# First expert product from 12-bit parts in short float32, b2 on TensorE, keys by transposes: one change to a fused token, attention and expert kernel

## The chip, the cores and the metric

The kernel runs on one core of a Trainium2 chip. The metric is the device time of one execution in microseconds (us). PE is TensorE, DVE VectorE, ACT ScalarE, POOL GpSimd, SP SyncE, which here only issues transfers. The matmul clock of PE has two levels, 1.2 and 2.4 GHz.

## What is computed

Sixteen images (3 x 112 x 112) become 50 tokens each (49 patches and a class token) of width D = 192, through a patch convolution, a wavelet branch and depthwise convolutions. With 128 text tokens each sequence has T = 178 tokens. Then two residual layers follow:

```python
h = h + attn(layernorm(h))            # 12 heads of 16, own token masked, softmax
h = h + ffn(layernorm(h))
# ffn: logits = gamma * zscore_last(q @ k.T * scale); probs = softmax(logits)
x = layernorm(src + probs @ v @ Wo.T + bo) * ln1_g + ln1_b
gate = softmax(x @ Wg.T + bg)         # 4 experts
combine = gate where it is among the two largest, else 0
hid = relu(x @ W1[e] + b1[e])         # 192 -> 768, for every expert e
y = hid @ W2[e] + b2[e]               # 768 -> 192
out = layernorm(x + sum_e combine[e] * y[e]) * ln2_g + ln2_b
```

All four experts are computed for every token; combine weighs them. Everything is to hold to about float32, since the choice of the two largest gates hangs on it.

## The kernel before, in words

**Stages.** A first block (0 to 156 us) makes the image tokens of all 16 images. The second block works on eight pairs of images. A pair's 2 x 178 tokens lie in three tiles of 128 partitions, the third with the 2 x 50 image tokens; transposed they are 370 columns (XN) of two halves of 96 rows (HC).

**Rounds.** A round works on three or four pairs at once: a in the second part of attention of layer 1 (stage 0), b in the attention of the ffn (stage 1), nxt entering layer 1, and m, the pair before b, in its expert layer. Two rounds without m run first, then a loop of five (`Fori`), then two rounds written out with their own fill tables (FILL_A7, FILL_B7), and a last one that holds nothing but the expert layer of pair 7. Each engine has its own program of the same round and meets the others by semaphores. The order on PE in `pe_round` is: turn xn[1], query, key and value of stage 1, `pe_deviation`, the pass for the maxima and the exponential pass of stage 0, the pass for the maxima of stage 1, output of stage 0, exponential pass and output of stage 1, turn, query and key of nxt, what is left of the experts, the transposes of x2 (L930), value of nxt (L736), the gate (L940).

**The expert layer as fill.** An expert layer has 24 units of 128 hidden channels (UNITS, six for an expert). `MOE_STEPS` is 49: step 2u is the first product of unit u (L615: two float32 products with K = 96, W1 as weights, x2T as the moving side, into bank 4 or 5), step 2u + 1 is the second product of unit u - 1 (L627: three products of hid with w2, summed over an expert's six units in banks 6 and 7). ACT makes hid (L640, relu with b1) in between. DVE adds comb[e] times the sum into acc behind every sixth unit (`expert`, L650) and gives the banks back by y_used. The table FILL says how many steps stand at each named point of the round; the rest (`moe.rest()`) follow after the key of nxt. Steps are the same on every engine, and each engine does its own part of them in its own order.

**b2.** `MoeDve.start` (L667) sets acc to x2 plus the four rows of b2 weighted by comb, in twelve instructions, right behind xc.

**A float32 product.** In the trace each float32 matmul is two records of weight load and matmul; a transpose and a bfloat16 matmul are one.

**The round's end on DVE.** In `dve_round` stand in this order: output of stage 1 (L1260, L1263), the norm of x2 (14 small steps and the products with ln1_g and ln1_b), the norm of h1 (`dve_norm1`), the splits of q32 and k32 of nxt into three bfloat16 parts (L1107 to L1110), what is left of the experts (expert 3), value of nxt (L1117), `dve_gate` (L1269 and on: softmax and the choice of two), `finish` (L678 to L694: the last norm, into fin). The next round begins with the mean of xT[1] (L1180) and xc = xT[1] - mean (L1186), on which PE's key product of stage 1 waits.

**Deviation.** The z-score of the logits needs the sum over keys of the squared centred logit. `pe_deviation` makes the centred keys a second time with tokens on partitions (`pe_tokens`, L736, six float32 products), ACT copies them (kct, L1016 to L1018), PE forms G = K'K for each image (L855), DVE masks it by head (L1201), PE multiplies it with q (L861), DVE with q again (L1207), PE sums within heads (L867).

**Weights.** w1 and w2 (2304 KB each) are loaded by SP in the first block. POOL only copies: the image tokens of the next pair into h0 (L1347), h1 into its keeps. SP stacks the parts of q and k through DRAM (`stack`, L1380 and L1384) and the rows of maxima (L1390).

## Time and profile before

| what | us |
|---|---|
| three runs | 1362.61, 1373.47, 1376.96 |
| their median | 1373.47 |
| profiled execution, span from first to last instruction | 1371.2 |
| PE busy | 1171.5 |
| DVE busy | 698.9 |
| ACT busy | 432.5 |
| POOL busy | 52.9 |

The profiled execution is told by its span; no own time of it is printed beside that. Busy time of PE is the union of its matmul records, and the end of a record is modelled with its latency, so that from one start to the next is the better measure of what a group takes. The mean granted clock of PE over the span is 0.881 of full speed. Idle time in brackets names what ended it; "issue" is time in which the engine waited for nothing that the profile shows.

### The profile page before, as it was taken

Reading aid. Unit: us, or ns where it says so; the run is one execution under the profiler, and the core shown is the slowest. Engines: PE = TensorE matmul, PEld = TensorE weight load, DVE = VectorE, ACT = ScalarE, POOL = GpSimd, SP = SyncE. Lnnn points to the kernel's source line nnn. Section 1 sums busy time; section 2 is a strip of 40 time slices with the busy share of each in tenths; the row PEclk is TensorE's granted clock in tenths of the full one; section 3 lists DMA queues with packets and bytes.
Section 4 is the critical chain, followed back from the end, with each engine's and each line's share of the span. In section 5 each row is a group of like instructions: output and inputs, shape, how many; then the busy total and the mean of one; then the engine's idle time right before and its main releaser. Section 6 shows DMA issues by size and latency. Waiting matters only on the chain.

```text
span 1371.2 us, 19879 instructions
## 1 busy us (share of the span) xinstructions
PE 1171.5 (85%) x7172; PEld 790.7 (58%) x7172; DVE 698.9 (51%) x1981; ACT 432.5 (32%) x933; POOL 52.9 (4%) x89
## 2 busy tenths in 40 slices
PE   7798546586789998999899989998999999885996
PEld 4343324353457666757666766575667756662775
DVE  3467742544275357535743574466456652724242
ACT  1222103132324342434242425332533343241321
POOL 6101100000000000000000000000000000000000
PEclk9999656566789998999898999998999999996998
DMA  9200040232031204210421043004301520012000
GB/s 277 88 1 0 7 78 1 47 76 40 8 78 40 41 7 88 54 33 1 88 58 29 1 94 66 15 15 87 65 10 25 101 41 2 9 39 40 1 8 8
DMA packets 37991, 60.55 MB, mean 44 GB/s; under 512 B 4976, under 2 KB 30176, under 8 KB 37344
## 3 DMA queue, kind: packets, MB, share of 16 engines
q1 hardware_dynamic: 35504, 55.86, 19.4%
q10 hardware_dynamic: 2384, 3.30, 0.8%
q8 instruction: 66, 1.08, 0.4%
q14 instruction: 37, 0.30, 0.1%
HBM read 42.36 MB, written 16.34 MB: 43 GB/s over the span
## 4 chain that ended last, share of the span: by engine, by line
PE 55%; DVE 19%; issue 9%; ACT 4%; DMA 2%; SPq 1%; DVEq 0%; POOL 0%; ACTq 0%; POOLq 0%
PE PS L615 13%; PE PS L627 11%; PE PS L736 6%; PE PS L822 5%; PE PS L763 5%; PE PS L728 4%; DVE mx L1227 3%; PE PS L769 3%; PE PS L778 2%; PE PS L831 2%; ACT probs L994 1%; PE PS L837 1%; PE PS L855 1%; PE PS L867 1%; DVE rem L1108 1%
## 5 line engine op out<-in xcount | busy, mean ns | idle before, releaser
L615 PE MATMUL PS<-x2T,w 96*128 96x370 f32 x768 | 289.8, 504 | 7.2 <-issue 7.2
L627 PE MATMUL PS<-w,hid 128*128 128x192 f32 x1152 | 233.9, 342 | 7.9 <-ACT hid L640 7.6
L627 PEld LDWEIGHTS PS<-w,hid 128*128 128x128 f32 x1152 | 205.4, 201 | 47.3 <-issue 12.6
L640 ACT ACTIVATE hid<-PS,b 128x370 f32<-128x370 f32 x192 | 108.8, 568 | 383.0 <-PE PS L615 383.0
L1227 DVE TENSOR_REDUCE mx<-PS 128x2 f32<-128x356 f32 x288 | 129.8, 520 | 148.5 <-PE PS L763 105.4
L615 PEld LDWEIGHTS PS<-x2T,w 96*128 96x128 f32 x768 | 146.9, 201 | 68.5 <-issue 18.8
L994 ACT ACTIVATE probs<-PS 128x356 f32<-128x356 f32 x288 | 112.8, 485 | 29.5 <-PE PS L763 19.3
L763 PE MATMUL PS<-kst,qst 96*128 96x178 bf16 x384 | 69.5, 276 | 32.8 <-DMA kst<-scr_k 14.2
L728 PE MATMUL PS<-xT,w_at 96*96 96x370 f32 x192 | 77.1, 552 | 8.8 <-ACT q L961 5.2
L778 PE MATMUL PS<-masks,ident_bf 128*128 128x256 bf16 (+1 forms) x288 | 79.8, 278 | 0.0
L650 DVE SCALAR_TENSOR_TENSOR acc<-PS,comb,acc 128x192 f32<-128x192 f32 x96 | 34.0, 409 | 86.9 <-PE PS L627 86.9
L822 PE MATMUL PS<-probs,va 128*32 128x178 f32 x1536 | 71.4, 328 | 6.7 <-ACT probs L994 6.7
L763 PE MATMUL PS<-qst,kst 99*128 99x178 bf16 x384 | 57.4, 252 | 17.2 <-DMA qst<-mrows 13.2
L1248 DVE RECIPROCAL rs<-PS 128x36 f32<-128x36 f32 x16 | 6.1, 383 | 129.2 <-PE PS L831 129.2
L763 PEld LDWEIGHTS PS<-kst,qst 96*128 96x128 bf16 x384 | 27.5, 105 | 67.0 <-DVE mx L1227 31.1
L736 PE MATMUL PS<-w_at,oT 96*128 96x192 f32 x288 | 55.8, 347 | 4.4 <-ACT oT L1011 4.4
L728 PEld LDWEIGHTS PS<-xT,w_at 96*96 96x96 f32 x192 | 35.2, 187 | 42.0 <-issue 10.6
L822 PEld LDWEIGHTS PS<-probs,va 128*32 128x32 f32 x1536 | 46.4, 112 | 22.1 <-issue 8.3
L736 PEld LDWEIGHTS PS<-w_at,oT 96*128 96x128 f32 x288 | 50.6, 202 | 8.5 <-ACT oT L1011 8.4
L763 PEld LDWEIGHTS PS<-qst,kst 99*128 99x128 bf16 x384 | 28.7, 101 | 44.8 <-issue 30.0
L371 DVE SCALAR_TENSOR_TENSOR dwo<-pad_l,chan,dwo 96x441 f32<-96x441 f32 x48 | 38.1, 793 | 14.1 <-ACT cw L295 12.6
L736 PE MATMUL PS<-w_at,xT 96*128 96x192 f32 x192 | 40.2, 366 | 5.5 <-ACT k L976 3.5
(190 smaller groups left out, 1393.0 us busy)
## 6 DMA issues: line engine op xcount, KB each, us to landing
qst<-scr_q SPq DMA_DIRECT2D x96, 144.0 KB, 4.6
scr_q<-qs SPq DMA_DIRECT2D x16, 432.0 KB, 3.3
scr_k<-ks SPq DMA_DIRECT2D x16, 432.0 KB, 4.7
kst<-scr_k SPq DMA_DIRECT2D x16, 432.0 KB, 4.8
w<-in_w SPq DMA_DIRECT2D x2, 2304.0 KB, 36.8
kst<-scr_k SPq DMA_DIRECT2D x16, 288.0 KB, 5.8
cols<-in_x_cols SPq DMA_DIRECT2D x6, 392.0 KB, 14.2
kst<-scr_k SPq DMA_DIRECT2D x16, 144.0 KB, 6.3
```

Of the source, the lines that this page charges most:

```text
L371: ch.link(nc.vector.scalar_tensor_tensor(out=out, in0=image_rows(PAD_OF[r][:, 0, :], tap_offset(t), n), scalar=col(C_DW + 18 * r + t), in1 ...
L615: ins = nc.tensor.matmul(PS[:, 4 + u % 2, 0:XN], w1[:, k, 128 * u:128 * u + 128], x2T[:, k, 0:XN], start=(k == 0), stop=(k == 1))
L627: ins = nc.tensor.matmul(tile_psum((6, 7), i), hid[u % 2][:, 128 * i:128 * i + 128], w2[:, u, :], start=(j == 0 and i != 1), stop=(j == FT ...
L640: nc.scalar.activation(hid[u % 2][:, 0:XN], PS[:, 4 + u % 2, 0:XN], ACT.Relu, bias=b1[:, u:u + 1]).then_inc(S["h_ready"], 1)
L728: ins = nc.tensor.matmul(PS[0:HC, FRONT[s][m], 0:XN], w_at[:, w, k, HC * m:HC * m + HC], x[:, k, 0:XN], start=(k == 0), stop=(k == 1))
L736: ins = nc.tensor.matmul(tile_psum(banks, i), tile_cols(x, k, i), w_at[:, w, k, :], start=(k == 0), stop=(k == 1))
L763: ins = nc.tensor.matmul(PS[:, bank, T * b:T * b + T], still[0:rows_, h, TP * b:TP * b + NTXT], move[0:rows_, h, TP * b:TP * b + T], start ...
L769: ins = nc.tensor.matmul(PS[64 * b:64 * b + 64, 2, T * g:T * g + T], still[0:rows_, 2 * u + g, TP * b + NTXT:TP * b + TP], move[0:rows_, 2 ...
L778: ins = nc.tensor.matmul(own, ident_bf[:], m.rearrange("p (b j) -> p b j", b=2), start=False, stop=True, skip_group_check=True)
L822: ins = nc.tensor.matmul(PS[32 * q:32 * q + 32, 3, T * b:T * b + T], va[s][:, 2 * i + b, h, :], pr, start=(i == 0), stop=(i == 1), skip_gr ...
L994: nc.scalar.activation(probs[:, u % PROB_UNITS, bank, :], PS[:, bank, 0:T2], ACT.Exp)\
L1227: nc.vector.tensor_reduce(out, PS[:, g, 0:T2].rearrange("p (b j) -> p b j", b=2), AX.X, ALU.max)\
```

## The change

x2 is transposed to full 128 partitions: plane 0 has channels 0 to 127, plane 1 has channels 128 to 191 twice (x2_wide holds those 64 columns a second time). ACT copies the transposes to x2T_hi in the type float32r (short float32), DVE writes the remainder as x2T_lo. W1 is held as w1_hi and w1_lo (channels 0 to 127) and w1_rest (rows 0 to 63 the high part of channels 128 to 191, rows 64 to 127 their low part). A unit's first product is then five short products over 128 rows. POOL makes these tiles at the start of the second block from loads that it issues itself, in four chunks of 1536 columns, by way of qst[1]; SP's stacks of stage 1 and PE's expert rounds wait for them. The gate takes the same parts, four products for a tile in place of two, and DVE adds the two halves.

b2 goes to PE: comb is transposed (bank 4), copied by ACT into hid[0], and multiplied with b2 in banks 6 and 7, which DVE adds to acc after expert 3. MOE_STEPS is 50.

The centred keys with tokens on partitions come from eight transposes of k32 in place of `pe_tokens`. The weights of the value product have 17 columns in place of 32, and DVE clears bank 3 once. tok_gain, tstat, tmv, tsc, loc, kct and gsb lie in other tiles now; tok_gain is loaded by SP at the start of the second block, and DVE waits for it. FILL and its two variants are unchanged.

```diff
-        w1 = sb("w1", [HC, 2, E * FF])
+        w1_hi = sb("w1_hi", [128, E * FF], F32R)
+        w1_lo = sb("w1_lo", [128, E * FF], F32R)
+        w1_rest = sb("w1_rest", [128, E * FF], F32R)
...
-        va = [sb(f"va{s}", [128, 4, HEADS, 32]) for s in range(2)]
...
                 pe, m = self.eng, self.m
-                if odd:
+                if u == UNITS and odd:
+                    self.bias()
+                elif odd:
                     if u:
                         self.second(u - 1)
                 elif u == UNITS:
+                    pe.wait_ge(S["comb_ready"], at(m, 1, 1))
+                    for i in range(3):
+                        ins = nc.tensor.transpose(PS[0:E, 4, 128 * i:128 * i + 128], comb[:, i, :], ident[:])
+                    ins.then_inc(S["ct_psum"], 1)
                     self.second(UNITS - 1)
                 else:
                     if u >= 2:
                         pe.wait_ge(S["h_ready"], at(m, UNITS, u - 1))
-                    for k in range(2):
-                        ins = nc.tensor.matmul(PS[:, 4 + u % 2, 0:XN], w1[:, k, 128 * u:128 * u + 128],
-                                               x2T[:, k, 0:XN], start=(k == 0), stop=(k == 1))
+                    f = slice(128 * u, 128 * u + 128)
+                    for k, (w, x, plane) in enumerate(((w1_hi, x2T_hi, 0), (w1_lo, x2T_hi, 0), (w1_hi, x2T_lo, 0),
+                                                       (w1_rest, x2T_hi, 1), (w1_rest, x2T_lo, 1))):
+                        ins = nc.tensor.matmul(PS[:, 4 + u % 2, 0:XN], w[:, f], x[:, plane, 0:XN],
+                                               start=(k == 0), stop=(k == 4))
                     ins.then_inc(S["h_psum"], 1)
+
+            def bias(self):
+
+                pe, m = self.eng, self.m
+                pe.wait_ge(S["y_used"], at(m, E + 1, E))
+                pe.wait_ge(S["ct_ready"], at(m, 1, 1))
+                for i in range(3):
+                    ins = nc.tensor.matmul(tile_psum((6, 7), i), combT[:, 128 * i:128 * i + 128], b2[:],
+                                           start=(i != 1), stop=True, skip_group_check=True)
+                ins.then_inc(S["bias_psum"], 1)
...
                     nc.scalar.activation(hid[u % 2][:, 0:XN], PS[:, 4 + u % 2, 0:XN], ACT.Relu,
                                          bias=b1[:, u:u + 1]).then_inc(S["h_ready"], 1)
+                elif not odd:
+                    act.wait_ge(S["ct_psum"], at(m, 1, 1))
+                    nc.scalar.copy(combT[:, 0:XN], PS[0:E, 4, 0:XN]).then_inc(S["ct_ready"], 1)
 
         class MoeDve(Moe):
 
 
             def expert(self, e):
                 dve, m = self.eng, self.m
+                if e == 0:
+                    dve.wait_ge(S["comb_ready"], at(m, 1, 1))
                 dve.wait_ge(S["h_used"], at(m, UNITS, FT * (e + 1)))
                 for i in range(3):
                     ins = nc.vector.scalar_tensor_tensor(out=acc[:, i, :], in0=tile_psum((6, 7), i),
-                                                         scalar=comb[:, i, e:e + 1], in1=acc[:, i, :],
+                                                         scalar=comb[:, i, e:e + 1], in1=(acc if e else x2)[:, i, :],
                                                          op0=ALU.mult, op1=ALU.add)
                 ins.then_inc(S["y_used"], 1)
-                dve.wait_ge(S["y_used"], at(m, E, e + 1))
+                dve.wait_ge(S["y_used"], at(m, E + 1, e + 1))
+
+            def bias(self):
+                dve, m = self.eng, self.m
+                dve.wait_ge(S["bias_psum"], at(m, 1, 1))
+                nc.vector.tensor_tensor(acc[:, 0:2, :], PS[:, 6, 0:2 * D].rearrange("p (i d) -> p i d", i=2), acc[:, 0:2, :],
+                                        ALU.add)
+                nc.vector.tensor_tensor(acc[:, 2, :], PS[:, 7, 0:D], acc[:, 2, :], ALU.add).then_inc(S["y_used"], 1)
+                dve.wait_ge(S["y_used"], at(m, E + 1, E + 1))
 
             def step(self, u, odd):
-                if u and u % FT == 0 and (odd or u == UNITS):
+                if u == UNITS and odd:
+                    self.bias()
+                elif u and u % FT == 0 and (odd or u == UNITS):
                     self.expert(u // FT - 1)
-
-            def start(self):
-
-                dve, m = self.eng, self.m
-                ch = chain(dve, "dve_bias", m)
-                dve.wait_ge(S["comb_ready"], at(m, 1, 1))
-                for e in range(E):
-                    for i in range(3):
-                        ins = nc.vector.scalar_tensor_tensor(out=acc[:, i, :], in0=rows[:, R_B2 + e, :],
-                                                             scalar=comb[:, i, e:e + 1], in1=acc[:, i, :] if e else x2[:, i, :],
-                                                             op0=ALU.mult, op1=ALU.add)
-                    ch.link(ins)
-                ch.end()
 
             def finish(self):
...
+                        ins = nc.tensor.matmul(PS[32 * q:32 * q + VW, 3, T * b:T * b + T], va[s][:, 2 * i + b, h, :],
                                                pr, start=(i == 0), stop=(i == 1), skip_group_check=True)
             ins.then_inc(S["pv_psum", s], 1)
...
 
-            pe_tokens((0, 1), 5, xc, S["kc_psum"])
+            for h in range(2):
+                for b_ in range(2):
+                    o = D * b_ + HC * h
+                    nc.tensor.transpose(PS[:, 0, o:o + HC], k32[:, h, b_, 0:NTXT], ident[0:HC, 0:HC])
+                    ins = nc.tensor.transpose(PS[0:NB, 1, o:o + HC], k32[:, h, b_, NTXT:T], ident[0:HC, 0:HC])
+            ins.then_inc(S["kc_psum"], 1)
             moe.point("kc")
             pe.wait_ge(S["kc_ready"], at(b, 1, 1))
             pe.wait_ge(S["v_ready", 1], at(b, 1, 1))
-            for c in range(2):
-                for h in range(2):
-                    for i in range(2):
-                        x = kct[:, 2 * i + c, HC * h:HC * h + HC]
-                        o = HC * (2 * h + c)
-                        ins = nc.tensor.matmul(PS[0:HC, 2, o:o + HC], x, x, start=(i == 0), stop=(i == 1))
+            for h in range(2):
+                for i in range(2):
+                    for c in range(2):
+                        half = slice(HC * h, HC * h + HC)
+                        x = kct[0:NB, 2 + c, half] if i else kct[:, c, half]
+                        ins = nc.tensor.matmul(PS[0:HC, 2 + c, half], x, x, start=(i == 0), stop=(i == 1))
             ins.then_inc(S["g_psum"], 1)
             moe.point("g")
             pe.wait_ge(S["g_ready"], at(b, 1, 1))
             for h in range(2):
                 for c in range(2):
-                    ins = nc.tensor.matmul(PS[0:HC, h, T * c:T * c + T], gsb[:, 2 * h + c, :], q32[1][:, h, c, 0:T],
+                    ins = nc.tensor.matmul(PS[0:HC, h, T * c:T * c + T], gsb[:, 2 * c + h, :], q32[1][:, h, c, 0:T],
...
+            if m is not None:
+                pe.wait_ge(S["w_split"], 2 * WCH + 1)
             moe.point("start")
...
-                        ins = nc.tensor.transpose(PS[0:HC, (2, 3)[h], 128 * i:128 * i + 128], x2[:, i, HC * h:HC * h + HC],
-                                                  ident[:])
+                        ins = nc.tensor.transpose(PS[:, (2, 3)[h], 128 * i:128 * i + 128],
+                                                  x2_wide[:, i, 128 * h:128 * h + 128], ident[:])
                 ins.then_inc(S["x2T_psum"], 1)
             if nxt is not None:
                 pe_value(pe, 0, nxt)
             if b is not None:
 
-                pe.wait_ge(S["x2T_ready"], at(b, 1, 1))
+                pe.wait_ge(S["w_split"], 1)
+                pe.wait_ge(S["x2T_lo"], at(b, 1, 1))
                 for i in range(3):
-                    for k in range(2):
-                        ins = nc.tensor.matmul(PS[:, 2, E * i:E * i + E], tile_cols(x2T, k, i), gate_w[:, k, :],
-                                               start=(k == 0), stop=(k == 1))
+                    o = 2 * E * i
+                    for k, (x, plane) in enumerate(((x2T_hi, 0), (x2T_lo, 0), (x2T_hi, 1), (x2T_lo, 1))):
+                        w = gate_b[:] if plane else gate_a[:].rearrange("p c e -> p (c e)")
+                        ins = nc.tensor.matmul(PS[:, 2, o:o + (E if plane else 2 * E)], tile_cols(x, plane, i), w,
+                                               start=(k == 0), stop=(k == 3), skip_group_check=True)
                 ins.then_inc(S["gate_psum"], 1)
 
...
             nc.scalar.copy(kct[:, 0:2, :].rearrange("p i d -> p (i d)"), PS[:, 0, 0:2 * D])
-            nc.scalar.copy(kct[0:NB, 2, :], PS[0:NB, 1, 0:D])
-            nc.scalar.copy(kct[64:64 + NB, 3, :], PS[64:64 + NB, 1, 0:D]).then_inc(S["kc_ready"], 1)
+            nc.scalar.copy(kct[0:NB, 2:4, :].rearrange("p i d -> p (i d)"), PS[0:NB, 1, 0:2 * D]).then_inc(S["kc_ready"], 1)
...
-                nc.scalar.copy(x2T[:], PS[0:HC, 2:4, 0:XW]).then_inc(S["x2T_ready"], 1)
+                nc.scalar.copy(x2T_hi[:], PS[:, 2:4, 0:XW]).then_inc(S["x2T_ready"], 1)
                 act.wait_ge(S["gl_ready"], at(b, 1, 1))
...
-                ch.link(nc.vector.tensor_tensor(y[:], y[:], row(gain, 3), ALU.mult))
-                ins = nc.vector.tensor_tensor(y[:], y[:], row(gain + 1, 3), ALU.add)
+                ch.link(nc.vector.tensor_tensor(y, y, row(gain, 3), ALU.mult))
+                ch.link(nc.vector.tensor_tensor(x2_wide[:, :, D:D + DB], y[:, :, 128:D], row(gain + 1, 3)[:, :, 128:D],
+                                                ALU.add))
+                ins = nc.vector.tensor_tensor(y, y, row(gain + 1, 3), ALU.add)
             ins.then_inc(done, 1)
...
-            moe.start()
             moe.point("norm")
             moe.point("query")
...
-            nc.vector.tensor_tensor(gsb[:], PS[0:HC, 2, 0:4 * HC].rearrange("p (i c) -> p i c", i=4),
-                                    same_head[:].unsqueeze(1).to_broadcast([HC, 4, HC]), ALU.mult).then_inc(S["g_ready"], 1)
+            for c in range(2):
+                ins = nc.vector.tensor_tensor(gsb[:, 2 * c:2 * c + 2, :], PS[0:HC, 2 + c, 0:D].rearrange("p (h c) -> p h c", h=2),
+                                              same_head[:].unsqueeze(1).to_broadcast([HC, 2, HC]), ALU.mult)
+            ins.then_inc(S["g_ready"], 1)
             moe.point("g")
...
-            nc.vector.tensor_tensor(gl[:], PS[:, 2, 0:3 * E].rearrange("p (i e) -> p i e", e=E),
-                                    bg[:].unsqueeze(1).to_broadcast([128, 3, E]), ALU.add).then_inc(S["gate_used"], 1)
+            parts = PS[:, 2, 0:6 * E].rearrange("p (i c e) -> p i c e", c=2, e=E)
+            ch.link(nc.vector.tensor_tensor(gl[:], parts[:, :, 0], bg[:].unsqueeze(1).to_broadcast([128, 3, E]), ALU.add))
+            nc.vector.tensor_tensor(gl[:], parts[:, :, 1], gl[:], ALU.add).then_inc(S["gate_used"], 1)
             dve.wait_ge(S["gate_used"], at(b, 1, 1))
...
+            if b is not None:
+                dve.wait_ge(S["x2T_ready"], at(b, 1, 1))
+                nc.vector.tensor_tensor(x2T_lo[:], PS[:, 2:4, 0:XW], x2T_hi[:], ALU.subtract).then_inc(S["x2T_lo"], 1)
             if nxt is not None:
                 dve_value(dve, 0, nxt)
...
+        def split_weights(pool):
+
+            for g in range(2):
+                out = gate_b[:] if g else gate_a[:, 0, :]
+                nc.gpsimd.tensor_copy(out, gate_w[:, g, :]).then_inc(S["w_cast"], 1)
+                pool.wait_ge(S["w_cast"], g + 1)
+            nc.gpsimd.tensor_tensor(gate_a[:, 1, :], gate_w[:, 0, :], gate_a[:, 0, :], ALU.subtract).then_inc(S["w_cast"], 1)
+            pool.wait_ge(S["w_cast"], 3)
+            nc.gpsimd.tensor_tensor(gate_b[DB:128], gate_w[DB:128, 1, :], gate_b[DB:128], ALU.subtract).then_inc(S["w_split"], 1)
+            for n in range(2 * WCH):
+                rest, f = n // WCH, slice(WC * (n % WCH), WC * (n % WCH) + WC)
+                pool.wait_ge(S["w_split"], n + 1)
+                pool.dma_start(raw, a["w1_rest" if rest else "w1"][:, f]).then_inc(S["raw_in"], 16)
+                pool.wait_ge(S["raw_in"], 16 * n + 16)
+                hi = (w1_rest if rest else w1_hi)[:, f]
+                nc.gpsimd.tensor_copy(hi, raw).then_inc(S["w_cast"], 1)
+                pool.wait_ge(S["w_cast"], n + 4)
+                if rest:
+                    ins = nc.gpsimd.tensor_tensor(w1_rest[DB:128, f], raw[DB:128], w1_rest[DB:128, f], ALU.subtract)
+                else:
+                    ins = nc.gpsimd.tensor_tensor(w1_lo[:, f], raw, hi, ALU.subtract)
+                ins.then_inc(S["w_split"], 1)
+            pool.wait_ge(S["w_split"], 2 * WCH + 1)
...
+            if s:
+                sp.wait_ge(S["w_split"], 2 * WCH + 1)
             sp.wait_ge(S[f"{which}_split", s], at(r, 1, 1))
...
                 load_text(sp, 0)
...
+                pe.wait_ge(ld_moe, 16)
                 pe.wait_ge(casts, 1)
...
                 for x in (qs, ks):
```

Outside of the engines' programs: w1 is laid out as its first 128 rows and, as w1_rest, its last 64 rows twice; gate_w likewise; b2 is an input of its own and no longer part of rows.

## Rows read from the trace of the kernel before

**Rows 1.** The page: busy shares; the chain that ended last, by engine and line

```profile
PE 1171.5 (85%) x7172; PEld 790.7 (58%) x7172; DVE 698.9 (51%) x1981; ACT 432.5 (32%) x933; POOL 52.9 (4%) x89
...
PE 55%; DVE 19%; issue 9%; ACT 4%; DMA 2%; SPq 1%; DVEq 0%; POOL 0%; ACTq 0%; POOLq 0%
PE PS L615 13%; PE PS L627 11%; PE PS L736 6%; PE PS L822 5%; PE PS L763 5%; PE PS L728 4%; DVE mx L1227 3%; PE PS L769 3%; PE PS L778 2%; PE PS L831 2%; ACT probs L994 1%; PE PS L837 1%; PE PS L855 1%; PE PS L867 1%; DVE rem L1108 1%
```

**Rows 2.** Groups by form: line, shapes, count; busy us, mean ns; idle before

```profile
L615 PE MATMUL PS<-x2T,w 96*128 96x370 f32 x768 | 289.8, 504 | 7.2 <-issue 7.2
...
L667 DVE SCALAR_TENSOR_TENSOR acc<-rows,comb,acc 128x192 f32<-128x192 f32 x72 | 27.7, 439 | 0.9
...
L1110 DVE TENSOR_TENSOR qs<-rem,qs 96x712 bf16<-96x712 f32 x16 | 14.4, 898 | 0.6
...
L340 POOL TENSOR_TENSOR dwo<-dwo,cw 96x441 f32<-96x441 f32 x10 | 13.6, 1365 | 101.8 <-ACT cw L295 101.8
```

**Rows 3.** Timeline of PE, 630 to 702 us: start, us, instruction, records, [idle before]

```profile
649.16 1.41 PE L615 MATMUL PS<-x2T,w 96*128 96x370 f32 x4
650.41 2.12 PE L627 MATMUL PS<-w,hid 128*128 128x192 f32 x12
652.36 0.82 PE L930 MATMUL PS<-ident,x 128*96 128x128 f32 x6
653.02 2.12 PE L736 MATMUL PS<-w_at,xT 96*128 96x192 f32 x12
...
658.20 4.42 PE L615 MATMUL PS<-x2T,w 96*128 96x370 f32 x8 [1.84 <-issue]
...
676.20 5.25 PE L728 MATMUL PS<-oT,w_at 96*96 96x370 f32 x8 [3.77 <-DVE oT L1186]
```

**Rows 4.** Busy time by stretch: us, then PE, PEld, DVE, ACT, POOL; clock, DMA

```profile
636.00:676.00 40.00, 34.59 (x157) 25.37 (x155) 30.61 (x107) 11.80 (x25) 1.32 (x2) 0.96 0.36 75
676.00:768.00 92.00, 87.49 (x661) 59.80 (x662) 42.19 (x116) 35.65 (x81) 0.69 (x2) 0.91 0.17 33
```

**Rows 5.** Timeline of DVE, 630 to 702 us

```profile
654.68 1.06 DVE L650 SCALAR_TENSOR_TENSOR acc<-PS,comb,acc 128x192 f32<-128x192 f32 x3
...
656.99 0.17 DVE L1269 TENSOR_TENSOR gl<-PS,bg 128x12 f32<-128x12 f32 x1
...
673.25 0.68 DVE L1180 TENSOR_REDUCE xbar<-xT 96x4 f32<-96x512 f32 x1 [6.00 <-issue]
```

**Rows 6.** Timelines of DVE and PE, last three rounds

```profile
1073.62 0.42 DVE L1186 TENSOR_TENSOR oT<-xT,xbar 96x256 f32<-96x256 f32 x1
...
1076.30 2.65 PE L728 MATMUL PS<-oT,w_at 96*96 96x370 f32 x8
...
1250.83 0.75 PE L763 MATMUL PS<-kst,qst 96*128 96x178 bf16 x4 [12.01 <-issue]
...
1315.27 1.07 DVE L667 SCALAR_TENSOR_TENSOR acc<-rows,comb,x 128x192 f32<-128x192 f32 x3
...
1321.21 1.21 PE L627 MATMUL PS<-w,hid 128*128 128x192 f32 x6 [0.19 <-DVE acc L650]
```

**Rows 7.** Timelines of PE and of SP's queue, 555 to 610 us

```profile
575.41 0.49 PE L796 MATMUL PS<-ident,mpart 128*36 128x128 f32 x3 [0.62 <-DVE mpart L1236]
...
580.30 0.31 PE L763 MATMUL PS<-qst,kst 99*128 99x178 bf16 x2
...
601.29 2.67 PE L615 MATMUL PS<-x2T,w 96*128 96x370 f32 x4
...
576.48 2.36 SPq L1390 DMA_DIRECT2D qst<-mrows  x3
```

**Rows 8.** The chain, in order of time: the same step in the first round

```profile
215.73 2.05 DMA qst<-mrows
```

**Rows 9.** DMA issues: bytes of one, us from issue to landing

```profile
bands<-in_pg_bands SPq DMA_DIRECT2D x1, 576.0 KB, 5.3
```

**Rows 10.** Timeline of POOL

```profile
243.76 0.34 POOL L1347 COPY h<-img_tok 49x192 f32<-49x192 f32 x1 [81.95 <-DVE h L1263]
```

73 lines of the change are left out of this document (45 added, 28 removed).

## The prediction

> **What bounds the kernel now.** I read the page's busy shares first: TensorE (PE) is busy 85% of the span, VectorE (DVE) 51%, and the chain that ended last is 55% PE and 19% DVE, its largest line L615, the first expert product, 13% [rows 1]. So one could think that every microsecond taken from L615 is won. The groups price it: 192 units of four matmul records, 289.8 us in all [rows 2]. In the timeline the next matmul starts 1.25 us after such a unit (649.16 to 650.41), so a record streams for 0.31 us and a float32 product, two records, takes 0.62 [rows 3].
>
> Then I asked where the chain runs, round by round. A steady round (132 to 138 us) has two parts. In the first, 92 us, PE is busy 87.5 and sets the pace [rows 4]. In the second, 40 us, from stage 1's output projection to the centred keys of the next round, the chain is DVE's: x2's norm, h1's norm, four splits, expert 3, value, gate, the end of the previous pair's expert layer, 6 us in which it issues nothing (the loop's turn), then the mean and xc [rows 5]. PE only fills there and waits 3.77 us for xc, after which it runs at the lower clock level (1.2 GHz): eight records of 370 columns take 5.25 us, at the upper level 2.65 [rows 3, 6]. What PE saves in this part is worth nothing; what DVE's chain gets longer there, the round does too. That split decides the case.
>
> **The first product.** Two float32 products (1.25 us) become five short ones of the same 370 columns. No row shows the short type. From below, a product can't be cheaper than one pass over its columns, half a record, 0.155 us; from above, it could run like float32, 0.62. I take one pass, as bfloat16 does: two records of 178 columns last 0.31 us together, their latency included [rows 7]. Loads of float32 weights follow each other every 0.11 us in the six transposes from 652.36 to 653.02 [rows 3], so they stay hidden. Five passes are 0.78 us: 0.47 saved a unit, 0.92 at the lower clock, where a unit has 2.67 less the latency, 2.47 [rows 7].
>
> The Trainium skill (FP8 and Floating Point Precision, TensorE Precision Notes) says that true FP32 takes four passes through the array, and that "FP32 reduced precision" reads four bytes and truncates them. The trace agrees with the four, 0.62 being 4 x 0.155; no run here shows the other. By one pass of it the sum is the one below, by float32's own rate it would be the far end of rival B.
>
> Of the 24 units of a steady round nine stand in DVE's part: nothing. Of the other fifteen, three are cover that is wanted anyway: one before the split maxima (PE waits 0.62 us for mpart even now), two before the exponential pass. There SP issues the rows of maxima at 576.48, three issues in 2.36 us, the last lands some 2 us after it starts [rows 7, 8], so near 580.2, and the pass starts at 580.30. Three more gain 0.1 to 0.2 us each, because something else is late next: rem, the residual, the copy of oT. One runs at the lower clock: 0.9. Eight are won whole: 3.7. Together 5.1 a round, 25.5 for five steady rounds. The two rounds behind the loop, counted the same way, give 5.2 and 5.6: in the second PE waits 12 us for its query stack at 1250.83 whatever the units before it cost [rows 6].
>
> **Keys by transposes.** Twelve records of L736, 1.95 us (as from 653.02, less the latency), go. Eight transposes come, four at 0.11 and four of 50 columns, between 0.03 and 0.11, taken at 0.06: 0.7. Saved 1.25 a round, twice that in the slow first one: 11. ACT has two copies for three, inside the expert steps that cover them, and G's mask is 0.15 longer on DVE, also covered.
>
> **b2 on TensorE.** Twelve DVE instructions of 0.44 us go, 5 us with their gaps [rows 2]. In steady rounds they stand behind xc, beside PE's key product, and cost nothing now. In the last round they are on the chain, from 1315.27, ahead of expert 0 and of PE at 1321.21 [rows 6]. What comes stands in the bad part. PE's bias step waits for DVE's expert 3, and DVE gets to that only behind its splits, at 655.7 [rows 5], while PE is done with its second products at 652.4 [rows 3], and after the change at 650.9 (four units shorter, three small transposes more). Behind the waiting bias stand on PE the transposes of x2, the next pair's value product and the gate, which today run while DVE splits. Worked out on this round's times: expert 3 ends at 656.1, 0.35 later for the extra piece of x2's norm. Then on PE bias 1.0, transposes 0.65, value 1.95; beside them ACT's copy 0.8, DVE's two adds 0.9 and the new low part of x2, 128x768, 0.95 after the 0.90 of a 96x712 op [rows 2]; then the gate 1.35. At the upper clock the gate's first DVE op starts at 661.5 instead of 656.99, and has one op more: 4.8 late. But by then PE has stood idle for 5 us, and after 3.77 and after 1.84 us it came back at the lower level [rows 3]. If bias, transposes and value all run there, it is 8.4. I take 7.0: the clock comes back within the value product. From there DVE's chain to xc is unchanged. Four boundaries at 7.0; the next, where PE is last today (xc at 1074.0, PE at 1076.30 [rows 6]), 4.9; the one after 7.0; the first, with no expert layer in flight, 1.8: 41.7 us.
>
> **Last round.** Its gate is 1.9 us late, start() is gone, so PE's seventh second product comes 1.7 earlier than 1321.21; 17 more units save 7.9; PE waits some 0.5 us for DVE at two expert boundaries, comb's transposes take 0.5, and the bias stands bare before the final norm, 1.15 on PE and 0.95 on DVE. Net 6.0 saved.
>
> **Start.** Clearing a PSUM bank on DVE costs 0.6. The weights come in four loads of 768 KB beside the stacking transfers: between 0 and 5, taken 1. Their split runs on POOL: a load of 7 us (576 KB took 5.3), a copy and a subtraction of 1536 elements, 4.8 each at L340's 3.1 ns for an element (441 in 1.37 us): 16.6 a chunk, done near 228, ahead of POOL's image at 243.76 [rows 2, 9, 10] and of SP's second stack, later still. 17 weight columns for 32 in the value product: loads are hidden, 0 to 7 us gained, taken 0.
>
> **Sum:** -25.5 - 10.8 - 11 - 6.0 + 41.7 + 1.6 = -10 us. The page gives the profiled execution by its span alone, 1371.2; what lies around it I take as the 2.3 us to the middle of the three runs: 1371.2 - 10 + 2.3 = 1363.
>
> **Rivals.** A, the boundary is cheap: PE's clock holds through the wait (4.8, 2.7 and 4.8 instead of 7.0, 4.9 and 7.0) and the marginal units gain too. Boundaries 28.5, gains 57, start 1.6: -27, 1347; with no cost of the bias wait at all, 1.5 a boundary, 1327. For it: at 658.20, after 1.84 us, the clock was back within three units. Against: the idle is 5 us. B, a short product is two passes long, 0.31: a unit takes 1.54, 0.3 longer than now. It decides as soon as a short product costs more than 0.25. Some 123 units lie on PE's part of the chain: +37, the slow ones +2, boundaries +42, transposes -11, last round's start() -4, start +1.6: +68, 1441. For: a float32 record itself is two passes. At float32's rate it would be some 300 us. C, POOL's split is late. Beyond 16 us of room each microsecond delays the next pair's image, which is on the chain: with loads of 15 us, 16 late, 1379.
>
> The Trainium skill (SBUF — State Buffer, SBUF: two separate sides) says that a load issued by GpSimd starves while VectorE runs a two-port copy. No row of this trace shows such a load; it is what would bring C about.
>
> D, the boundary is dearer, 8.4 each, and the units in the exponential passes gain half, because ACT's exponentials come late: boundaries 50, gains 45, start 1.6: +7, 1380.
>
> **How the numbers follow.** A change of this kernel can be told from none beyond about 1%, 13.7 us. Forecast 0.40, A 0.30, B 0.07, C 0.07, D 0.16. All of A and a third of the forecast's case end below 1359.8: 0.42. All of B and two thirds of D: 0.18. The rest, 0.40, is within 1%. The range goes from between A's two values, 1335, to D's far side, 1388.
>
> **What would show it.** The first product has 960 records, 0.16 us apart. In a steady boundary PE idles 5 us before the bias, and DVE's gate starts some 8 us behind the end of expert 3, not 1.3. L667 is gone; PE is busy near 1070 us in a hardly shorter span. Wrong would be: records 0.3 us apart (B), a gap before POOL's image near 244 (C), a steady round under 130 us (A) or above 138 (D).

## The result, and the profile after

The changed kernel takes 1377.81 us (median of 20 runs), the kernel before 1371.45 beside it: ratio 1.0070, 95% interval 1.0041 to 1.0099, slower by 0.7% (by the two medians 0.5%). The forecast was 1363 us and a gain; the time came out on the other side of the kernel before. The profiled execution has a span of 1382.0 us for 1371.2. In what follows 0.001 of a ratio is 1.37 us. The ratios leave out runs more than 1.5% above the fastest of the same kernel, which matters for two kernels below: one run of six of e4, at 3394 us, and five of twelve of e13, at 1379 to 1382 us.

The page of the changed kernel:

```profile
span 1382.0 us, 20370 instructions
PE 1129.3 (82%) x7404; PEld 834.5 (60%) x7404; DVE 690.9 (50%) x1934; ACT 436.2 (32%) x933; POOL 78.9 (6%) x105
...
PE 51%; DVE 22%; issue 8%; ACT 4%; DMA 3%; SPq 1%; DVEq 0%; POOL 0%; ACTq 0%; POOLq 0%
...
L638 PE MATMUL PS<-x2T_hi,w_hi 128*128 128x370 f32 x192 | 93.4, 486 | 4.4 <-issue 4.4
...
L638 PE MATMUL PS<-x2T_hi,w_lo 128*128 128x370 f32 x192 | 67.6, 352 | 0.0
```

Against [rows 1], PE is busy 42 us less, not the 101 us that the forecast meant by 1070, and DVE 8 us less. Then the timeline of PE where products stand among second products at the upper clock (start, us, records):

```profile
1043.79 1.14 PE L660 MATMUL PS<-w,hid 128*128 128x192 f32 x6
1044.63 0.47 PE L638 MATMUL PS<-x2T_hi,w_hi 128*128 128x370 f32 x1
1044.93 0.33 PE L638 MATMUL PS<-x2T_hi,w_lo 128*128 128x370 f32 x1
1045.10 0.33 PE L638 MATMUL PS<-x2T_lo,w_hi 128*128 128x370 f32 x1
1045.27 0.33 PE L638 MATMUL PS<-x2T_hi,w_rest 128*128 128x370 f32 x1
1045.43 0.33 PE L638 MATMUL PS<-x2T_lo,w_rest 128*128 128x370 f32 x1
1045.60 1.14 PE L660 MATMUL PS<-w,hid 128*128 128x192 f32 x6
```

A short product is one pass, 0.17 us from start to start: rival B falls. But the second record comes 0.30 behind the first, since the first takes over from a float32 product (0.45 behind a projection of 96 rows, at 1053.26). A first and a second product take 1.81 us together (1043.79 to 1045.60) where [rows 3] have 2.22: 0.41 saved, not 0.47.

A steady boundary, PE first, then DVE:

```profile
664.78 2.04 PE L648 MATMUL PS<-b,hid 4*128 4x192 f32 x6 [4.79 <-DVE acc L688]
...
673.06 0.25 PE L982 MATMUL PS<-gate_b,x2T_lo 128*128 128x4 f32 x1
...
689.57 2.73 PE L760 MATMUL PS<-oT,w_at 96*96 96x370 f32 x8 [2.53 <-DVE oT L1231]
```

```profile
663.66 1.06 DVE L688 SCALAR_TENSOR_TENSOR acc<-PS,comb,acc 128x192 f32<-128x192 f32 x3
666.93 0.56 DVE L697 TENSOR_TENSOR acc<-PS,acc 128x384 f32<-128x384 f32 x1 [2.21 <-PE PS L648]
...
669.23 0.96 DVE L1383 TENSOR_TENSOR x2T_lo<-PS,x2T_hi 128x768 fp32r<-128x768 f32 x1 [1.48 <-ACT x2T_hi L1119]
...
673.35 0.17 DVE L1316 TENSOR_TENSOR gl<-PS,bg 128x12 f32<-128x12 f32 x1
...
686.16 0.68 DVE L1225 TENSOR_REDUCE xbar<-xT 96x4 f32<-96x512 f32 x1 [2.36 <-issue]
```

This is what was forecast: PE idles 4.79 us ahead of the bias product, comes back at the lower level (2.04 us for six records; the value product takes 3.99 us for the 2.12 of [rows 3]), and DVE's gate starts 8.6 us behind the end of expert 3 instead of 1.3. But DVE's idle time at the loop's turn, 6.00 us in [rows 5], is 2.36 here. Over four turns it was 24.6 us and is 9.3. And PE waits 2.53 us for xc, not 3.77, and the key product behind it runs at the upper level, 2.73 us for the 5.25 of [rows 3]. At the four boundaries of the loop this product took 4.24, 5.25, 2.73 and 5.25 us before, and takes 2.65 to 2.73 now.

By the copies of the pairs' images on POOL the kernel loses 6.2 us up to the first (249.99 for 243.76 [rows 10]), 3.7 in the round after it and 1.6 in the next; the four steady rounds gain 1.85 each (133.0 for 134.85); the first stretch behind the loop loses 6.4, the next two 4.3 and 0.4, and the last layer gains 4.5.

### The profile page after: what moved, and what is told of

It is laid out like the page before. It is cut to its first block, busy times and chain, and to the rows that moved or that the text cites. A ratio compares the mean times of both kernels' runs of the same rounds, so it can differ in the third digit from the quotient of the medians.

```text
span 1382.0 us, 20370 instructions
## 1 busy us (share of the span) xinstructions
PE 1129.3 (82%) x7404; PEld 834.5 (60%) x7404; DVE 690.9 (50%) x1934; ACT 436.2 (32%) x933; POOL 78.9 (6%) x105
## 4 chain that ended last, share of the span: by engine, by line
PE 51%; DVE 22%; issue 8%; ACT 4%; DMA 3%; SPq 1%; DVEq 0%; POOL 0%; ACTq 0%; POOLq 0%
PE PS L660 10%; PE PS L638 8%; PE PS L768 6%; PE PS L854 5%; PE PS L795 5%; DVE mx L1273 4%; PE PS L760 3%; PE PS L801 3%; PE PS L810 2%; PE PS L863 1%; PE PS L982 1%; DMA qst<-mrows 1%; PE PS L892 1%; PE PS L648 1%; SPq L1464 1%
## 5 line engine op out<-in xcount | busy, mean ns | idle before, releaser
L660 PEld LDWEIGHTS PS<-w,hid 128*128 128x128 f32 x1152 | 201.7, 199 | 16.1 <-ACT hid L673 5.3
L638 PE MATMUL PS<-x2T_hi,w_hi 128*128 128x370 f32 x192 | 93.4, 486 | 4.4 <-issue 4.4
L854 PE MATMUL PS<-probs,va 128*17 128x178 f32 x1536 | 70.5, 326 | 6.8 <-ACT probs L1036 6.8
L638 PE MATMUL PS<-x2T_hi,w_lo 128*128 128x370 f32 x192 | 67.6, 352 | 0.0
L638 PE MATMUL PS<-x2T_lo,w_rest 128*128 128x370 f32 x192 | 67.5, 351 | 0.0
L638 PE MATMUL PS<-x2T_lo,w_hi 128*128 128x370 f32 x192 | 67.2, 350 | 0.0
L638 PE MATMUL PS<-x2T_hi,w_rest 128*128 128x370 f32 x192 | 67.2, 350 | 0.0
L854 PEld LDWEIGHTS PS<-probs,va 128*17 128x17 f32 x1536 | 41.1, 99 | 24.6 <-issue 5.7
L688 DVE SCALAR_TENSOR_TENSOR acc<-PS,comb,acc 128x192 f32<-128x192 f32 x72 | 25.5, 409 | 58.1 <-PE PS L660 58.1
L768 PE MATMUL PS<-w_at,xT 96*128 96x192 f32 x192 | 49.9, 430 | 5.5 <-ACT k L1018 3.4
```

Of the source, the lines that this page charges most:

```text
L638: ins = nc.tensor.matmul(PS[:, 4 + u % 2, 0:XN], w[:, f], x[:, plane, 0:XN], start=(k == 0), stop=(k == 4))
L660: ins = nc.tensor.matmul(tile_psum((6, 7), i), hid[u % 2][:, 128 * i:128 * i + 128], w2[:, u, :], start=(j == 0 and i != 1), stop=(j == FT ...
L688: ins = nc.vector.scalar_tensor_tensor(out=acc[:, i, :], in0=tile_psum((6, 7), i), scalar=comb[:, i, e:e + 1], in1=(acc if e else x2)[:, i ...
L768: ins = nc.tensor.matmul(tile_psum(banks, i), tile_cols(x, k, i), w_at[:, w, k, :], start=(k == 0), stop=(k == 1))
L854: ins = nc.tensor.matmul(PS[32 * q:32 * q + VW, 3, T * b:T * b + T], va[s][:, 2 * i + b, h, :], pr, start=(i == 0), stop=(i == 1), skip_gr ...
```

## The experiments

Each of the ratios is against the kernel before, run on the same chip; in brackets the 95% interval. The changed kernel has 1.0070.

**The start.** On DVE and POOL, changed kernel:

```profile
169.58 3.48 POOL L1419 TENSOR_TENSOR w_lo<-qst,w_hi 128x1536 fp32r<-128x1536 f32 x1
169.63 3.45 DVE L144 TENSOR_SCALAR acc<-acc 128x7 int32<-128x7 int32 x1
...
178.25 1.91 POOL L1414 CAST w_hi<-qst 128x1536 fp32r<-128x1536 f32 x1 [4.32 <-DMA qst<-in_w]
178.87 2.70 DVE L1209 TENSOR_TENSOR img_tok<-img_tok,fin 128x1344 f32<-128x1344 f32 x1
180.24 4.70 POOL L1419 TENSOR_TENSOR w_lo<-qst,w_hi 128x1536 fp32r<-128x1536 f32 x1
181.49 3.84 DVE L1150 CAST qs<-q 96x712 bf16<-96x712 f32 x1
```

DVE's shift of seven numbers lasts as long as POOL's subtraction, and its cast of the queries 3.84 us.

```diff
 def split_weights(pool):
+    pool.wait_ge(S["k_split", 0], 1)
```

> The changed kernel, with POOL's split of the weights held back until DVE has split the first pair's keys; nothing else differs. Theory (POOL's casts and subtractions hold up DVE's own casts and scalar operations at the start): the three long DVE operations of the start (3.37, 2.70 and 3.77 us in the changed kernel) come back to 0.1, 1.6 and 0.5 us, the first max pass starts near 201 instead of 208, the next pair's image is copied near 244 to 246 instead of 249.99, and the whole is 5 to 7 us shorter than the changed kernel (1.007 of before becomes 1.002 to 1.003). Rival (the weight loads beside the stacking transfers cost it, or PE's clock): the three operations get short but the first max pass stays near 206 to 208. Rival (POOL late after all): the split, 52 us long, ends near 248 and the image copy waits for it, so nothing is won.

1373.85 us, 1.0035 [1.0006, 1.0065]. DVE's three operations in this run:

```profile
174.93 0.16 DVE L144 TENSOR_SCALAR acc<-acc 128x7 int32<-128x7 int32 x1
...
180.88 1.56 DVE L1209 TENSOR_TENSOR img_tok<-img_tok,fin 128x1344 f32<-128x1344 f32 x1
182.35 0.52 DVE L1150 CAST qs<-q 96x712 bf16<-96x712 f32 x1
```

From the first block's last addition into the image tokens to POOL's first image copy it is 89.6 us (159.07 to 248.68), in the kernel before 89.5, in the changed kernel 96.8. The weight loads now stand beside the stacking transfers and cost nothing, and the split ends at 234.6, 14 us ahead of the copy. So it is POOL's arithmetic that cost the start, 7 us in this stretch of the trace. The whole kernel's ratio falls by 5 us, which is no more than the two intervals allow by chance; the stretch and the three operations decide it. The copy's mark itself came at 248.68, later than expected, since in this execution everything ahead of POOL's split was already 5 to 6 us late.

The Trainium skill (SBUF — State Buffer, SBUF: two separate sides) calls the ports shared by VectorE and GpSimd "an exclusive lock, not a bandwidth split", held by whichever starts first. The trace agrees: POOL's subtraction starts at 169.58, DVE's operation at 169.63, and it takes 3.45 us for 0.16. The forecast had used that section only for DVE holding up POOL.

**The bias step.** Banks 4 and 5 are free once the last hidden units are read, so the product needn't wait for expert 3. DVE then reads it from there, and the next pair's first unit waits until DVE has:

```diff
-                pe.wait_ge(S["y_used"], at(m, E + 1, E))
                 pe.wait_ge(S["ct_ready"], at(m, 1, 1))
+                pe.wait_ge(S["h_ready"], at(m, UNITS, UNITS))
...
-                    ins = nc.tensor.matmul(tile_psum((6, 7), i), ...
+                    ins = nc.tensor.matmul(tile_psum((4, 5), i), ...
```

> The changed kernel, with the bias product put into PSUM banks 4 and 5 so that it doesn't wait for DVE's expert 3; the order of all instructions is kept. Theory (the wait ahead of the bias step is what makes the boundary dear): PE goes on at once, DVE's gate starts 4 to 5 us earlier behind the end of expert 3 (3.3 to 4.6 us behind it instead of 8.6). The two boundaries outside the loop gain 4 to 5 us each. In the loop DVE's gap at the turn was 6.15 us each before and 2.3 after the change: if it is tied to a fixed point of the round it grows back by up to 3.7 and a boundary gains about 1, total -13 us against the changed kernel; if the gap stays 2.3, total -28. Rival (the low part of x2 and the gate's four products are the cost, not the wait): gain under 6 us in all.

1351.67 us, 0.9888 [0.9830, 0.9945]: 25 us below the changed kernel, with some 9 us either way. Its boundary, PE and then DVE:

```profile
657.56 1.24 PE L650 MATMUL PS<-b,hid 4*128 4x192 f32 x6
...
664.34 0.24 PE L984 MATMUL PS<-gate_a,x2T_hi 128*128 128x8 f32 x1 [2.78 <-DVE x2T_lo L1385]
```

```profile
661.29 1.06 DVE L690 SCALAR_TENSOR_TENSOR acc<-PS,comb,acc 128x192 f32<-128x192 f32 x3
...
665.85 0.17 DVE L1318 TENSOR_TENSOR gl<-PS,bg 128x12 f32<-128x12 f32 x1 [0.56 <-PE PS L984]
...
679.79 0.68 DVE L1227 TENSOR_REDUCE xbar<-xT 96x4 f32<-96x512 f32 x1 [3.48 <-issue]
```

The gate starts 4.6 us after expert 3 begins, not 9.7 (663.66 to 673.35). The gap at the turn grew back, but by 1.4 us (3.69 for 2.33, mean of four turns), not 3.7: a steady round takes 129.75 us for 133.0, and the two stretches behind the loop gain 6.5 and 4.8.

Next, DVE forms the low part of x2 ahead of expert 3:

```diff
+            if b is not None:
+                ... x2T_lo <- PS - x2T_hi
             moe.rest()
-            if b is not None:
-                ... x2T_lo <- PS - x2T_hi
```

> As the run before it, and DVE forms the low part of x2 ahead of expert 3 and the bias additions, so that PE's gate runs beside these. By the theory of the wait it gains another 2 to 2.5 us at each of seven boundaries where the turn's gap doesn't give it back: 5 us (gap grows) to 15 us (gap stays) below the run before it. Rival: DVE now waits for ACT's copy of x2 ahead of expert 3, and nothing is won.

1343.69 us, 0.9837 [0.9787, 0.9886]: 7 us less, in the lower part of what was expected, and less than the two intervals together. Steady rounds gain only 0.9 (128.85).

And b2 back on DVE, the rest of the change kept:

```diff
-MOE_STEPS = 2 * UNITS + 2
+MOE_STEPS = 2 * UNITS + 1
+            moe.start()    # behind xc: twelve acc <- rows * comb + acc
```

> The changed kernel with b2 back on VectorE (twelve operations behind the centred keys, as before), all four with the first expert's b2 (the other three are left out, the time is the same); no transposes of comb, no bias product. The first product and the key transposes stay. By the forecast's sum: each steady boundary loses the wait for expert 3 (about 5 us won on the gate), the last round gets its 5 us back on the chain. With the gap at the loop's turn growing back: -4 in the loop, -9 outside, +4 in the last round, so about -9 against the changed kernel; with a constant gap -24. If b2 were a gain, it would be slower than the changed kernel by up to 5.

1346.14 us, 0.9833 [0.9775, 0.9891]. b2 on TensorE costs 0.0237, 32 us, with some 9 us either way. Both of my sizes (-9 and -24) were too small: the gap at the turns stays short (2.64 to 3.48). The profiled executions place the cost: 4.4 us in each steady round (133.0 for 128.6), and 18.8 us from the last image copy to the end.

**The three repairs together.**

> The changed kernel with the late split of the weights, the bias product in banks 4 and 5, and the low part of x2 ahead of expert 3. If the two causes are separate, the gains add: e3 stood at 0.984 of before, the late split gave 0.0035 to 0.005 (5 to 7 us at the start), so 0.979 to 0.980, near 1340. If the start's delay was absorbed later, it stays 0.984.

1342.52 us, 0.9800 [0.9760, 0.9840]. As expected if the gains add; the step from e3, 5 us, is itself within the intervals.

**The parts of the change alone.** The keys by transposes, put into the kernel before:

> The kernel before with the transposed keys alone (eight transposes for twelve matmuls, two copies on ACT for three, the mask in two pieces on DVE). The forecast gave it -11: 1.25 us in each of seven rounds, twice that in the slow first one: ratio 0.992. Rival: where PE is not last (G waits for DVE's value in the rounds with an expert layer) most of it is lost: -3, ratio 0.998. Rival: less PE work makes the first rounds slower by the clock: ratio 1.0.

1363.96 us, 0.9968 [0.9937, 1.0000]: -4, not -11. The eight transposes are 0.66 us as forecast (682.40 to 683.06). But G's sixteen records, behind them, now take 1.94 us from the first start to the next instruction, 1.36 before. To see why, three more. G's products in the old order, which brings seven changes between 128 and 50 rows instead of three:

```diff
-for h in range(2):
-    for i in range(2):
-        for c in range(2):
+for c in range(2):
+    for h in range(2):
+        for i in range(2):
```

> The keys alone (e6, ratio 0.9968), with G's eight products in the order of the kernel before: both halves of the token sum behind each other in the same bank, instead of a change of bank at every product. In e6 the sixteen records of G follow each other every 0.12 us, before every 0.083, which gives back 0.58 of the 1.3 us that the transposes save. If the order makes them slow, the records come 0.083 apart again and the ratio falls by 0.003 to 0.993 to 0.994. If it is the 50-row halves of the tile, they stay 0.12 apart and the ratio 0.997.

1372.59 us, 1.0049 [1.0017, 1.0082]: my first theory (the order makes them slow) is wrong, and the second (the 50 rows, whatever their order) is only half of it. G takes 2.62 us. Not the 50 rows but each change of the number of rows costs: 0.58 us over three changes, 1.26 over seven, 0.18 to 0.19 us each. Then all eight over 128 rows, the rest of the tile being zero:

```diff
-x = kct[0:NB, 2 + c, half] if i else kct[:, c, half]
+x = kct[:, 2 * i + c, half]
```

> The keys alone (e6, ratio 0.9968), with G's eight products all over 128 rows: the image halves of the tile are zero from row 50 on, so the sums are the same. In e6 the sixteen records took 1.80 us from the first start to the last with three changes between 128 and 50 rows, in e9 2.5 us with seven changes, before 1.25 with none: 0.18 us a change. If the change of rows is the cost, the records come 0.083 apart again, G's group falls from 18.8 us of PE time in the whole run to 12.3, and the ratio goes to 0.993 to 0.995. If the change of banks or the transposed tile itself is the cost, they stay 0.12 apart.

1347.71 us, 0.9845 [0.9801, 0.9890]. G's groups, in the order e6, e9, e12 (busy us, mean ns):

```profile
L860 PE MATMUL PS<-kct 50*96 50x96 f32 x64 | 9.7, 275 | 0.0
L860 PE MATMUL PS<-kct 128*96 128x96 f32 x64 | 9.1, 267 | 1.5 <-DVE va L1125 1.4
```

```profile
L860 PE MATMUL PS<-kct 50*96 50x96 f32 x64 | 13.8, 298 | 0.0
L860 PE MATMUL PS<-kct 128*96 128x96 f32 x64 | 13.2, 290 | 1.5 <-DVE va L1125 1.4
```

```profile
L860 PE MATMUL PS<-kct 128*96 128x96 f32 x128 | 12.3, 249 | 1.5 <-DVE va L1125 1.4
```

The group falls from 18.8 to 12.3 us as expected, but the kernel by 17 us, about four times what was expected. With G left over 128 rows, the keys by transposes gain 21 us, and not the forecast's 11. And the narrow products alone, in the kernel before:

```diff
-x = kct[:, 2 * i + c, HC * h:HC * h + HC]
+x = kct[0:NB if i else 128, 2 * i + c, HC * h:HC * h + HC]
```

> The kernel before with nothing changed but the rows of G's image halves: 50 instead of 128 (the second entry's image rows are left out of G with that, the time is the same). Seven changes of rows in G's eight products, as in e9, which took 2.5 us for 1.25. Theory A: 0.18 us x 7 changes x 7 rounds = 9 us, ratio 1.006. Theory B: more than twice that, 1.013 or above. Rival (the narrow rows cost nothing, the transposes do): 1.000.

1376.56 us, 1.0048 [1.0013, 1.0082]: theory A, 6.6 us. G takes 2.62 us in a steady round, as in e9, here with no transposes ahead of it. Full rows in the changed and in the repaired kernel:

```diff
+kimg = img_tok[:, 0:2, :]
-x = kct[0:NB, 2 + c, half] if i else kct[:, c, half]
+x = kimg[:, c, half] if i else kct[:, c, half]
...
```

> The changed kernel with G's image halves summed over all 128 rows: their tile lies where the image tokens of the first two pairs are done with, cleared once by POOL. Nothing else differs. Theory A (each change between 128 and 50 rows costs 0.18 us and no more): G's records come 0.083 us apart again, 0.54 us less a round, ratio 1.007 becomes 1.004. Theory B (the narrow products cost more than their own time, as e12 against e6 showed: 0.0123 of the time): ratio 0.995.

1373.41 us, 0.9965 [0.9916, 1.0014], which would be theory B. But the twelve runs go from 1356.9 to 1382.0 us, and the ratio rests on seven of them; the median of all twelve, against 1367.82 for the kernel before, gives 1.004, which is theory A. This run does not decide between the two.

> The three repairs (e5, 0.980) with the same full rows. Theory A: 0.977. Theory B: 0.968, so about 1323 us.

1327.27 us, 0.9680 [0.9627, 0.9733]. This is the best kernel of the study, 3.2% faster than before. Here it is B, 0.012 below e5, and no run is left out of e5, e6, e12 or e14. So by these two pairs the narrow products cost 16 to 17 us where the transposes stand ahead of them (three changes a round), and by e15 7 without the transposes (seven changes). Three changes a round explain 4 to 5 of the former; why it is more was not found. The steady rounds show 0.9 to 2.4 us each (e12 132.3 for e6's 133.45; e13 132.1 for the changed kernel's 133.0; e14 126.6 for e5's 128.9). In e12 a further part lies in the first round, and is not cleanly this step's: that round took 102.9, 104.4, 109.6, 113.4 or 117 us in kernels whose first rounds are nearly alike (e13 102.9, e12 104.4, e6 109.6, e14 113.0, e5 113.4, the changed kernel 117.1), with a granted clock of 0.55 to 0.74 over 250 to 370 us. It goes mostly in lumps near 4 us. What selects the lump stays open.

The old order in the repaired kernel:

> The three repairs (e5, ratio 0.980) with G's products in the old order: 0.6 us less in each of seven rounds if e9's first theory holds, so 0.977; otherwise 0.980.

1344.41 us, 0.9836 [0.9800, 0.9871]: not better than e5, as e9 lets one expect (the difference, 5 us the other way, is within the intervals).

The first product alone:

> The first product from high and low parts, alone: b2 on VectorE (all four with the first expert's b2) and the centred keys from their own product as before (the image rows of the tile that G reads aren't cleared, so the deviations are not the reference's; the time is the same). By e4 (0.9833 with the keys by transposes) and the forecast's 11 us for these it comes out at 0.991; if the transposes are worth 3 us, at 0.9855.

1347.72 us, 0.9844 [0.9803, 0.9886], -21 us. And how many of its units count:

```diff
-((w1_hi, x2T_hi, 0), (w1_lo, x2T_hi, 0), (w1_hi, x2T_lo, 0), (w1_rest, x2T_hi, 1), (w1_rest, x2T_lo, 1))
+((w1_hi, x2T_hi, 0), (w1_hi, x2T_lo, 0), (w1_rest, x2T_hi, 1))
```

> The changed kernel with two of the five short products of each unit left out (the low part of the weights' first 128 rows, and the last 64 rows' cross terms with the low part), so that the output is less exact. It takes 0.33 us from each of 192 units, 64 us of PE. By the forecast's count (10.9 units' worth in each of five steady rounds, 23 in the two behind the loop, 17 in the last) 95 units are won: -31 us against the changed kernel. If every unit counts: -64. If the products are hidden by other waits: under -15.

1360.28 us, 0.9911 [0.9875, 0.9946]: 0.0159 or 22 us, with some 6 us either way, for 64 us of PE work. At 0.33 us a unit that is 66 units' worth where the forecast counted 95. And they aren't where the forecast had them. It had 54.5 of the 95 in the loop, but the four steady rounds of the profiled execution are no shorter, 133.8 us for 133.0. At each boundary in the loop PE now waits 2.5 to 3.8 us for xc, and the key product behind the wait runs at the lower level:

```profile
680.61 5.25 PE L759 MATMUL PS<-oT,w_at 96*96 96x370 f32 x8 [3.29 <-DVE oT L1230]
```

In the changed kernel it takes 2.73 us or less there. What the shorter units gave went into that wait and the lower clock behind it. The gain shows behind the loop (10.5 us), in the last layer (6.7) and in the first two rounds (10.1), the first of which holds no unit, so that its 3.5 us are one of the lumps told above.

**One unit moved into the boundary.**

```diff
-("exp", 1): (1, 0, 1, 1, 0, 2)
+("exp", 1): (1, 0, 1, 1, 0, 0)
```

> As the run before it, with one unit (1.8 us of PE) taken from the last pair of heads of stage 1's exponential pass in the steady rounds and left to the part where DVE's chain is the bound. PE idles some 3 us there ahead of the gate. The pass gets 1.8 us shorter, the low part of x2 comes up to 1 us later: 0.8 to 1.8 us a round, ratio lower by 0.003 to 0.006. If the unit was hidden in the pass (ACT's exponentials), it is the same or slower by up to 0.003.

1382.39 us, 1.0111 [1.0077, 1.0146], 38 us above e10; a steady round takes 136.6 us for e10's 129.6. PE:

```profile
646.97 2.29 PE L662 MATMUL PS<-w,hid 128*128 128x192 f32 x6 [7.01 <-DVE acc L690]
```

The moved unit took expert 2's end with it into DVE's norm of x2: the next second product waits 7.01 us for DVE's expert addition, and queries, keys, splits and the gate stand behind it. It is the bias step's wait once more, made by a number in a table, and I had not looked what the unit carries.

## Why the prediction was wrong

The forecast's sum by part beside the runs, in us. The forecast itself didn't split its boundaries; here the first product gets 1.5 for each of seven, rival A's price without the bias wait, and b2 the rest. Of the last round the first product gets its 17 units and b2 the rest.

| part | forecast | measured |
|---|---|---|
| b2 on TensorE | 31.2 in the boundaries, 1.9 in the last round: +33 | +32 (changed kernel less e4) |
| keys by transposes | -11 | -4 (e6) |
| first product: units -44, boundaries 10.5, start 1.6 | -32 | -21 (e8) |
| sum | -10 | +7; the changed kernel itself +9.6 (by medians +6.4) |

Each measured part carries 4 to 9 us either way, so the split is rough. The forecast failed in two terms of its sum: the units of the first product counted as won whole, and the keys by transposes, where the products that read the new tile were put at no cost. The start was a smaller miss. b2's term held.

- **The boundary** was the argument's centre and its mechanism holds: idle 4.79 us where 5 stood, the gate 7.3 us later where I took 7.0. That the totals agree, 33 and 32, is partly luck: in the loop b2 cost 4.4 us a round where 5.5 were forecast, and from the last image copy to the end 18.8 where 10.8 were (profiled executions of the changed kernel and e4). Behind the loop the price was too low: PE's last projection of the next boundary came 12.3 us later (1088.64 for [rows 6]'s 1076.30), of which 2.75 were there before it (DVE's output of stage 1, 1043.40 for 1040.65): 9.6, not 4.9. I had counted PE as last there with its work at full speed, but its first units ran at the lower level (1.7 and 1.5 us each, from 1073.23).
- **Keys by transposes** is the step that left a term out. "Saved 1.25 a round" counted what goes and what comes, and not the neighbour that changed its form: G's products over 50 rows beside such over 128 cost 0.18 us a change, and 16 to 17 us in all (e12, e14). Without them the transposes gain 21 us (e12), so the gain was mis-sized as well, the other way. Whether the changed kernel alone would have gained without them isn't shown: e13 stands at 0.9965 by seven runs and at 1.004 by the median of twelve.
- **Start, taken 1.6**, cost 5 (ratio of e1) to 7 (its trace). The search was for waits of POOL, not for what POOL's work does to DVE. Rival C named the place and had the sign of the dependence reversed: its time, 1379, is right by accident; POOL was ready in time, its split ending at 207.3 where the copy stood at 249.99.
- **Eight units won whole** in a steady round is the other step that failed. A unit gives 0.41, not 0.47, because the second record comes late where the first follows a float32 product, and 66 units count, not 95. The two give 27 us for the 44. By e7's trace the count is too high in the loop: PE work taken away there came back as a longer wait for xc and as a key product at the lower level. The forecast let PE's part of the round shrink freely and put at nothing the level at which PE comes back behind that wait. e7 takes work out of the changed kernel, not of the kernel before, so that the 66 are carried over to e8 and not measured there.
- **What helped, unforeseen:** DVE's gap at the loop's turn. With the first product alone it is 13.1 us over four turns (e8), before 24.6: -11.5. With this, e8's sum closes: -27 + 10.5 + 7 - 11.5 = -21. That the terms are these is worked out, not shown singly: the 10.5 are the forecast's own, and the key product at the upper level at all four boundaries, 6.6 us less than before, is in none of them, so that the closing is partly luck.
- Against the rivals: B is out (0.17 us a record); A's cheap boundary is out; D, at 1380, had the nearest reasons (boundaries above 7, part of the units' gain gone), though its cause for the second, late exponentials of ACT, was not tested.

## What to carry to other kernels

Ask of each step that is moved or added what it waits for and what stands behind it in its engine's order. Here a 1 us product that waited for DVE cost 32 us, and the same product in a free PSUM bank gives 25 of them back. PE work taken out ahead of a wait for another engine can give nothing: the wait grows, and the product behind it may run at the lower clock. Price that product too. When an operand gets a new shape, price the instructions that read it too, and keep neighbouring products on the same number of rows, if need be by zero rows. Work on GpSimd is not free beside VectorE: put it where VectorE waits.

## What the runs showed of the hardware that I had not expected

- A change between products of 128 and of 50 rows costs PE 0.18 to 0.19 us at the upper clock (1.94 us for G with three changes in e6, 2.62 with seven in e9 and e15, 1.36 with none in e12).
- A DVE operation of 0.16 us took 3.45 while POOL subtracted 1536 columns; an elementwise addition of two tensors took 2.70 for 1.56, a cast 3.84 for 0.52.
- DVE's idle time at the loop's turn, 5.5 to 6.8 us in kernels with the float32 first product, is 2.2 to 4.3 with the short one. Its cause was not found. Loads of instructions stand in the DMA queues at the turns (3 packets from 662 to 674 us before, 4 from 674 to 687 in the changed kernel); whether DVE waits for them was not tested.
- The key product behind the wait for xc took 5.25 us in all four loop boundaries of e7 and 2.65 to 2.73 in those of the changed kernel, with PE waits of 2.5 to 3.8 us and 0 to 2.5 us.
- The first round, with nearly the same work, took 103 to 117 us in different kernels, mostly in lumps of about 4 us, at a granted clock of 0.55 to 0.74. Single rounds of a profile say little at this size; ratios over many runs say more.
